# Softmax denominators broadcast by bf16 high and low halves instead of fp32 matmuls, and a third staging buffer for x

## The reference

```python
xn = _layernorm(x, axis=-1)
# attention
qkv = xn @ c_attn_w.T + c_attn_b
q, k, v = heads(q), heads(k), heads(v)
q_lat = q @ q2l_w.T + q2l_b
k_lat = k @ kv2l_w.T + kv2l_b
v_lat = v @ kv2l_w.T + kv2l_b
q_lat, k_lat = rope(q_lat), rope(k_lat)
q_for_k = q_lat @ wqk_w.T + wqk_b
att = jnp.einsum('bhql,bhkl->bhqk', q_for_k, k_lat) * L ** (-0.5)
att = softmax(where(causal, att, -inf))
y_lat = jnp.einsum('bhqk,bhkl->bhql', att, v_lat)
s = (y_lat @ l2o_w.T + l2o_b) @ cproj_w.T + cproj_b
# feed-forward, int32 weights scaled by 1/127
h = silu(xn @ wg.T) * (xn @ wu.T)
g = silu(h @ wd.T)
return x + s * g
```

## Time and profile before

| what | value |
|---|---|
| median of 3 runs | 1739.2 us |
| the profiled execution | 1736.67 us |
| its span on the core of the page | 1735.1 us |
| spans of the 8 cores | 1722.1 to 1735.1 us |
| TensorE matmul busy | 1360.3 us, 78% |
| VectorE busy | 606.1 us, 35% |
| ScalarE busy | 645.5 us, 37% |

### The profile page before, as it was taken

The page is one execution under the profiler, slowest core; times in us unless marked ns, Lnnn a source line. Parts: engine busy times, 40 slices in busy tenths (PEclk is TensorE's granted clock), DMA queues, the critical chain, the costliest instruction groups (busy, mean ns, idle before and its releaser), DMA issues.

```text
span 1735.1 us, 17888 instructions; the slowest of 8 cores (1722.1 to 1735.1 us)
## 1 busy us (share of the span) xinstructions
PE 1360.3 (78%) x5077; PEld 501.2 (29%) x5152; DVE 606.1 (35%) x1174; ACT 645.5 (37%) x1170; POOL 0.2 (0%) x4
## 2 busy tenths in 40 slices
PE   0135697587588587587688598879999999989998
PEld 0112222222222222222222222224444444434443
DVE  3436532532532532532532532321122222222322
ACT  1432254254254254263263255544333333320111
POOL 0000000000000000000000000000000000000000
PEclk9997855855755756756755755559999999999999
DMA  2221000000000000000000000001222222225553
GB/s 81 90 93 36 26 1 13 25 1 13 25 1 13 25 1 12 25 1 13 25 1 13 25 1 1 1 25 61 86 83 76 73 75 84 73 70 173 170 170 122
DMA packets 19074, 82.26 MB, mean 47 GB/s; under 512 B 2914, under 2 KB 3492, under 8 KB 15780
## 3 DMA queue, kind: packets, MB, share of 16 engines
q1 hardware_dynamic: 18980, 81.11, 14.4%
HBM read 72.72 MB, written 8.39 MB: 47 GB/s over the span
## 4 chain that ended last, share of the span: by engine, by line
PE 71%; DVE 19%; issue 5%; ACT 3%; DMA 1%; DVEq 1%; SPq 0%; ACTq 0%
PE SA L847 10%; PE PG L678 8%; PE PD L684 7%; PE SA L652 6%; PE PA L506 6%; PE PB L506 5%; PE SA L910 5%; PE PB L847 5%; PE PA L847 5%; PE SA L733 3%; PE SA L737 3%; PE PA L910 2%; PE PB L910 2%; PE PA L790 2%; PE PB L790 2%
## 5 line engine op out<-in xcount | busy, mean ns | idle before, releaser
L663 ACT ACTIVATE arena<-SA 128x512 bf16<-128x512 f32 (+1 forms) x320 | 170.6, 533 | 260.3 <-DVE arena L749 107.6
L678 PE MATMUL PG<-arena 128*64 128x512 bf16 (+1 forms) x320 | 180.8, 566 | 76.4 <-DVE arena L673 50.9
L652 PE MATMUL SA<-arena 32*128 32x512 bf16 (+1 forms) x320 | 167.5, 526 | 59.0 <-ACT arena L573 40.6
L684 PE MATMUL PD<-arena 128*64 128x512 bf16 (+1 forms) x320 | 177.7, 564 | 4.3 <-DVE arena L726 4.1
L847 PE MATMUL SA<-xnT,wbuf_b 128*128 128x512 bf16 x753 | 172.5, 379 | 0.8
L506 PE MATMUL PA<-xnT,arena 128*128 128x512 bf16 x369 | 100.9, 417 | 54.8 <-DVE arena L499 54.1
L670 DVE TENSOR_TENSOR arena<-arena,mask_b 128x128 bf16<-128x128 bf16 x128 | 28.5, 222 | 289.2 <-ACT arena L663 287.5
L652 PEld LDWEIGHTS SA<-arena 32*128 32x128 bf16 x320 | 31.3, 98 | 268.7 <-issue 268.5
L847 PEld LDWEIGHTS SA<-xnT,wbuf_b 128*128 128x128 bf16 x768 | 75.2, 98 | 90.6
L549 ACT ACTIVATE arena<-PA,blat_f 128x512 f32<-128x512 f32 x16 | 11.0, 687 | 242.6 <-PE PA L537 242.4
L461 PE MATMUL PT<-ident_b,rtmp 128*128 128x128 bf16 x128 | 16.2, 306 | 106.0 <-DVE rtmp L457 106.0
(11 more groups left out here) (123 smaller groups left out, 1651.2 us busy)
## 6 DMA issues: line engine op xcount, KB each, us to landing
arena<-wqkv SPq DMA_DIRECT2D x24, 512.0 KB, 4.1
wbuf_i<-wg SPq DMA_DIRECT2D x24, 512.0 KB, 3.7
arena<-wu SPq DMA_DIRECT2D x24, 512.0 KB, 3.6
arena<-wd SPq DMA_DIRECT2D x8, 1536.0 KB, 13.5
arena<-x SPq DMA_DIRECT2D x16, 512.0 KB, 4.3
xnT<-xT SPq DMA_DIRECT2D x8, 1024.0 KB, 9.3
out<-xnT SPq DMA_DIRECT2D x8, 1024.0 KB, 5.2
arena<-wcproj SPq DMA_DIRECT2D x8, 512.0 KB, 4.0
```

The lines of the kernel that those rows point to most:

```text
L652: E("tensor", lambda e, i=i, qoff=qoff, N=N, p=p, SAp=SAp: e.matmul(SAp[:, 0:N], aug_k[p][0:32, i * 128:(i + 1) * 128], aug_q[p][0:32, qof ...
L663: E("scalar", lambda e, N=N, ip=ip, SAp=SAp: e.activation(pt_A[ip][:, 0:N], SAp[:, 0:N], AF.Exp, scale=SCL), reads=[rSAp], writes=[rpa], i ...
L678: E("tensor", lambda e: e.matmul(PG[0:64, qoff - 512 * j:qoff - 512 * j + N], aug_v[p][:, i * 128:i * 128 + 64], pt_A[ip][:, 0:N], start=( ...
L684: E("tensor", lambda e: e.matmul(PD[0:64, qoff - 512 * j:qoff - 512 * j + N], aug_v[p][:, i * 128 + 64:(i + 1) * 128], pt_B[ip][:, 0:N], s ...
```

## The change

It has two parts.

The epilogue's broadcast. VectorE splits the 1024 fp32 reciprocals into a bf16 high half and a bf16 low half: a cast of `rsrow` to bf16 in the space of `ytmp_f` on partition 0, a subtraction that writes the low half to `hilo` on partition 64, and a copy of the high half to `hilo`. TensorE then broadcasts with four bf16 matmuls of one row, with a row of ones and zeros, `ones64_b`, as weights. All of it stands in `em_epi`, in the place of the two fp32 matmuls.

The staging of x. Layernorm tiles use three buffers in turn, `wf0`, `wf1` and `xstage3`, where `xstage3` lies over `wpb0` and `wpb1`.

```diff
+        ones64_b = alloc("ones64_b", [128, 256], BF16)
...
+        hilo = rsc[64:65, :].bitcast(BF16)
...
-        wpb0 = carve(1024)
-        wpb1 = carve(1024)
+        wpb01 = carve(2048)
+        wpb0 = wpb01[:, 0:1024]
+        wpb1 = wpb01[:, 1024:2048]
+        xstage3 = wpb01.bitcast(F32)
...
+        E("vector", lambda e: e.memset(ones64_b[64:65, 0:256], 0.0),
+          writes=[res("ones64")], inc="dv")
+        E("vector", lambda e: e.memset(ones64_b[64:65, 0:64], 1.0),
+          writes=[res("ones64")], inc="dv")
+        E("vector", lambda e: e.memset(ones64_b[64:65, 192:256], 1.0),
+          writes=[res("ones64")], inc="dv")
         for tt in range(NT):
-            bi = tt % 2
-            wfp = wf0 if bi == 0 else wf1
-            rwf = res("wf0" if bi == 0 else "wf1")
+            bi = tt % 3
+            wfp = (wf0, wf1, xstage3)[bi]
+            rwf = res(("wf0", "wf1", "wpbx")[bi])
...
                 def em_epi(g=g, j=j, rrs=rrs, rylr=rylr):
-                    E("tensor", lambda e: e.matmul(
-                        SA0[:], onesA_f[:], rsrow[:, 0:512],
-                        start=True, stop=False, skip_group_check=True),
-                      reads=[res("onesA"), rrs], writes=[rSA0], inc="pe")
-                    E("tensor", lambda e: e.matmul(
-                        SA0[:], onesB_f[:], rsrow[:, 512:1024],
-                        start=False, stop=True, skip_group_check=True),
-                      reads=[res("onesB"), rrs], writes=[rSA0], inc="pe")
+                    rhl = res("hilo")
+                    ryt0 = res("ytmp_f")
+                    hi0 = ytmp_f[0:1, :].bitcast(BF16)
+                    E("vector", lambda e, hi0=hi0: e.tensor_copy(
+                        hi0[:, 0:1024], rsrow[:, 0:1024]),
+                      reads=[rrs], writes=[ryt0], inc="dv")
+                    E("vector", lambda e, hi0=hi0: e.tensor_sub(
+                        hilo[:, 1024:2048], rsrow[:, 0:1024], hi0[:, 0:1024]),
+                      reads=[rrs, ryt0], writes=[rhl], inc="dv")
+                    E("vector", lambda e, hi0=hi0: e.tensor_copy(
+                        hilo[:, 0:1024], hi0[:, 0:1024]),
+                      reads=[ryt0], writes=[rhl], inc="dv")
+                    for mi, (sel, seg) in enumerate((
+                            (slice(0, 128), slice(0, 512)),
+                            (slice(0, 128), slice(1024, 1536)),
+                            (slice(128, 256), slice(512, 1024)),
+                            (slice(128, 256), slice(1536, 2048)))):
+                        E("tensor", lambda e, sel=sel, seg=seg, mi=mi: e.matmul(
+                            SA0[:], ones64_b[64:65, sel], hilo[:, seg],
+                            start=(mi == 0), stop=(mi == 3),
+                            skip_group_check=True),
+                          reads=[res("ones64"), rhl], writes=[rSA0], inc="pe")
```

More of the change, by code:

```diff
@@ L474, in build_nc @@
         alias_seed(res("rtmp1"), res("xn_b1"))
+        alias_seed(res("wpb0"), res("wpbx"))
+        alias_seed(res("wpb1"), res("wpbx"))
         ryT = res("yT")
```

## The result

The kernel after runs in 1774.3 us, the kernel before in 1736.7 us beside it: a ratio of 1.0218, 95% interval 1.0207 to 1.0229. It is slower. The profiled execution's span is 1771.9 us on its slowest core, 36.8 us over the 1735.1 of before.

What follows compares the result with a forecast made beforehand. TensorE was taken as the bound, with the stretch from last mask to L742 on the path 32 times. Epilogues +34.1 us and late weights +4.2 gave +38.3, so 1775 us, 2.2% slower; range 1756 to 1790.

Steps and rivals of the forecast that it cites:

- The split on VectorE: Epilogue: three VectorE instructions behind the last mask, unhidden; broadcast starts 2.69 us after it, not 0.42, a 2.27 us delay.
- The short split: Rival: subtraction and copy run at their lower ends, delay 1.51 us per epilogue; 1744 us, within 2%; chance 0.18.
- the hidden split: Rival: the three instructions run in VectorE's gaps earlier in the block, only dropped passes count; 1694 us; chance 0.04.
- late epilogues: 8 epilogues at 1.2 GHz after four-key-tile blocks, where the reciprocal ends late: +0.79 us each, +6.3 together.
- The matmuls: Epilogue broadcast: four bf16 matmuls replace two fp32 ones; 3.89 to 2.0 us at 1.2 GHz, 2.09 to 1.23 at 2.4.
- The epilogues at 1.2 GHz: 11 epilogues at half clock without a late reciprocal: 2.27 + 2.0 - 3.89 = +0.38 us each, +4.2 together.
- the 13 epilogues at 2.4 GHz: Epilogues whose broadcast had full clock: +18.6 us together if kept, +28.6 if it falls to 1.2 GHz; +23.6 taken.
- the rival that the clock is lost: All 13 full-clock broadcasts fall to 1.2 GHz: 1780 us, inside the forecast's 0.50; with a long split, chance 0.18.
- The staging: Layernorm's third x buffer: hides nothing, but group 0's q weights load late, first matmul 122.0 to 126.2 us, +4.2 us.
- the half chance of a kept clock: Full-clock epilogues: middle taken between broadcasts keeping 2.4 GHz, +1.43 us each, and falling to 1.2 GHz, +2.20 each.
- the longer ends of the split: Epilogue: split instructions at their upper times, 3.08 us in all, a delay of 2.66; with lost clock up to 1799 us.

Runs made afterwards that it cites:

- The late load alone: Kernel before with two x buffers, but group 0's q weights are loaded only once tile 15 is normalised: 1742.0 us, ratio 1.0026.
- the rotated buffers: Kernel before with three x buffers starting one further on, so tile 15 lies in the third, and the fp32 epilogue: 1737.6 us, ratio 1.0006.

## Why the prediction was right, point by point

- The split on VectorE was the term that decided, and it was sized right: 0.68, 1.22 and 0.42 us against 0.68, 1.22 and 0.45, and a broadcast that starts 2.68 us behind the last mask against 2.69. That it is on the path is shown from both sides: without it the kernel after runs 75 us faster, and it alone makes the kernel before 95 us slower. The short split falls with the row of L751, 1.217 us and not 0.69, and the hidden split with the timeline, where the cast stands right behind the last mask. Its price was too good as well: with the split emitted early the kernel ran in 1733 us and not in 1694, as the 8 late epilogues keep the split in their path and the masks of 8 blocks wait for it.
- The matmuls: 1.97 us at 1.2 GHz, where I took 2.0 out of 1.93 to 2.18. The epilogues at 1.2 GHz went from 4.31 to 4.65 us, +0.34 against +0.38.
- The late epilogues: 0.85 us longer (the broadcast starts 3.63 us behind the last mask and not 0.90, and is 1.9 us shorter) against +0.79.
- The clock: for the 13 epilogues at 2.4 GHz I took the middle between kept and lost, +23.6 us. It was nearly all lost. On the core of the page 26 of the 32 broadcasts take 1.96 to 1.97 us, one 1.12 and five between 1.27 and 1.72. Of the 13 epilogues that had full clock before, ten now run their broadcast at 1.2 GHz, one keeps the clock and two part of it; together they are 26.8 us longer, near the 28.6 of the rival that the clock is lost. The other three that have some full clock are among the 11 slow ones, which are therefore only 2.2 us longer in all and not 4.2. Windows of two epilogues of the kernel after (PE, PEld, DVE, ACT, POOL busy, PEclk), the first ahead of its idle wait and in its broadcast, the second in its idle wait, at the start of its broadcast and at the end of it:

```profile
235.00:236.00 1.00, 0.70 (x5) 0.26 (x3) 0.81 (x3) 0.26 (x2) 0.00 (x0) 1.00 0.00 0
239.00:240.00 1.00, 1.00 (x3) 0.14 (x1) 0.00 (x0) 0.00 (x0) 0.00 (x0) 0.50 0.00 0
...
423.50:424.50 1.00, 0.00 (x0) 0.00 (x0) 0.90 (x2) 0.00 (x0) 0.00 (x0) 1.00 0.00 0
425.10:425.60 0.50, 0.50 (x3) 0.19 (x3) 0.00 (x0) 0.00 (x0) 0.00 (x0) 1.00 0.00 0
425.70:426.40 0.70, 0.70 (x3) 0.10 (x1) 0.00 (x0) 0.00 (x0) 0.00 (x0) 0.50 0.00 0
```

  So the short stretches at full clock still come, 11 on this core where there were 13, but TensorE spends them on the end of the value matmuls and on its idle wait, and in all but one of them the clock is back at 0.50 before the broadcast is through. The Trainium skill's rule that activity releases the throttle ("TensorE: Matmul & The Clock Gate", What's actually happening) agrees with the fall behind the idle wait. The idle wait is not the whole of it: in the kernel without the split there is none, and only 3 to 9 of the broadcasts of a core are at 2.4 GHz, in the one with the early split 3 to 5. No run here separates the shorter broadcast from the shift of what stands around it, so why full clock gets rarer in them stays open.
- The staging: no gain in layernorm, and +3.9 us for the late q weights against +4.2; another 0.5 of the +4.4 is start-up scatter. The late load alone costs 0.26%, the rotated buffers nothing that can be told. That the staging part alone costs 0.68% was not priced: its slowest cores had 6 epilogues at full clock, and the slowest before had 10 to 13. In the kernel after little of this can show, since there few broadcasts have full clock in either case.
- Sum: 34.1 + 4.2 predicted, 34.0 + 4.4 measured to the end of attention, and 1.6 us less in the stages behind. That it agrees to 0.1 us is partly luck. The epilogues themselves grew by 35.9 us: 26.8 in the 13 at full clock, 2.2 in the 11, 6.9 in the 8 late ones. The stretches between them, which the prediction took as unchanged, gave 1.9 back, each by at most 1.1 us either way. The mechanism and the sizes of its steps are right; the half chance of a kept clock is what the trace does not bear out, and it was 5 us of the sum.
- One bound does not follow: the 1799 us of the lost clock "with the longer ends of the split". The split's longer end adds 0.39 us to each of 32 epilogues, 12.5 us to 1780; 1799 needs the matmuls' 2.18 and the load's 5.2 at their longer ends too. The upper end of the range hung on it, and the result does not come near.

Open: why some cores of the staging part alone have 11 or 12 epilogues at full clock and others 6 or 7. The late load by itself, with nearly the same shift, left all cores at 12 or more, so the shift alone did not do it there, and the rotated buffers, with the third buffer and no shift, left all cores at 10 or more. No run here tells what does.

## What to carry to other kernels

When work is moved from the busiest engine to an idle one, look at what stands between the two in each engine's list: 2.3 us on an idle VectorE in front of a matmul cost 75 us where the halved matmul saved some 41. The same instructions a few key tiles earlier cost 34 us: nothing where VectorE has a gap, as much as before where the reciprocal comes late, and 1 us where masks stand close behind. A matmul with one row uses one of 128 rows: laying two rows on two partitions of one tile halved the matmuls too, with nothing put in front. Look for a wait for a load before adding a third buffer; here there was none after the first tile, and the rotation decided which buffer came free last.

## What was not expected of the hardware

- The clock stayed at 0.50 all through the 3.9 us of back-to-back one-row fp32 matmuls from 512.30 to 516.20. On the core shown of the kernel before, each of the 32 broadcasts took either 2.06 to 2.11 us or 3.85 to 3.88, and nothing between.
- The cores of one program in one execution can differ by 9 to 11 us through how many of 32 short broadcasts meet the full clock: 6 or 12 in the staging part alone, 10 or 16 in the kernel before.
- A cast on one partition takes as long as on 128: 0.676 us for 1 x 1024 and 0.684 for 128 x 1024. So does a copy out of PSUM: 0.682 us for 1 x 512 (L705) and 0.692 for 128 x 512 (L742). The subtraction on one partition has no row on 128 of its length beside it.
